# FFN rows of a graph transformer block: stores issued by ScalarE and SyncE instead of by Pool

## What is computed

```python
xn = _layernorm(x)
x = x + gnn(xn, edges) + mix(xn)          # two attentions, 16 heads each
y = _layernorm(x)
q, k, v = (_fff(y, *w[f]) for f in "qkv")  # three routed feed-forward nets
x = x + softmax(q @ k.T / sqrt(1024)) @ v
# _fff: a tree of depth 4 gives each row one of 16 leaves;
# hidden = relu(y @ w1[leaf] + b1[leaf])   (64 wide)
# out    = hidden @ w2[leaf] + b2[leaf]    (1024 wide)
```

## Time and profile before

| | us |
|---|---|
| median of 3 runs | 715.43 (714.16 to 717.3) |
| the profiled execution | 715.37 |
| its span, first to last instruction | 713.6 |
| PE busy | 689.6 |
| DVE busy | 478.7 |
| ACT busy | 404.2 |
| Pool busy | 247.7 |

### The profile page before, as it was taken

How to read it: one execution, slowest core, us unless ns; L and a number is a source line. 1 busy time by engine, 2 the same in 40 slices (tenths; PEclk the granted TensorE clock), 3 DMA queues, 4 the chain that set the end, 5 groups by cost and what they waited for, 6 DMA issues and landing times.

```text
span 713.6 us, 11638 instructions
## 1 busy us (share of the span) xinstructions
PE 689.6 (97%) x4371; PEld 650.6 (91%) x4371; DVE 478.7 (67%) x965; ACT 404.2 (57%) x702; POOL 247.7 (35%) x232
## 2 busy tenths in 40 slices
PE   3999999999999999999999999999999899989998
PEld 3999999998999999999999999998899797879896
DVE  6778756784777477766667565658675667786744
ACT  5655646565565464768686775422432666675541
POOL 5744212122232232127022274564007831252240
PEclk9999999999999999999999999999999999999999
DMA  6822463432333223231313152333168879897342
GB/s 252 314 113 99 198 235 123 175 102 81 121 111 112 99 80 119 96 115 60 118 60 107 72 193 73 130 122 118 60 236 285 303 281 346 325 371 292 117 155 97
DMA packets 25096, 115.38 MB, mean 162 GB/s; under 512 B 7249, under 2 KB 7681, under 8 KB 15969
## 3 DMA queue, kind: packets, MB, share of 16 engines
q1 hardware_dynamic: 14144, 85.05, 32.5%
q0 software_dynamic: 10464, 29.39, 11.7%
q10 hardware_dynamic: 432, 0.20, 0.1%
HBM read 99.35 MB, written 22.49 MB: 171 GB/s over the span
## 4 chain that ended last, share of the span: by engine, by line
PE 85%; DVE 6%; ACT 4%; DMA 3%; issue 1%; ACTq 0%; POOLq 0%; DVEq 0%
PE g_bank L1923 35%; PE g_bank L1948 12%; PE o_bank L2000 5%; PE t_bank L1989 4%; PE s_bank L2280 2%; PE s_bank L1977 2%; PE s_bank L1978 2%; DVE w_lo L1265 2%; PE s_bank L2561 2%; PE s_bank L2508 2%; PE s_bank L2510 2%; PE g_bank L1877 2%; PE s_bank L2509 2%; PE t_bank L2363 2%; PE t_bank L2280 2%; DMA ys<-y_ring 1%
## 5 line engine op out<-in xcount | busy, mean ns | idle before, releaser
L1923 PE MATMUL g_bank<-act_hi,w_hi 128*128 128x384 f32 x488 | 169.3, 347 | 0.2 <-DVE v_st L1292 0.2
L1923 PE MATMUL g_bank<-act_hi,w_lo 128*128 128x384 f32 x488 | 163.6, 335 | 0.0
L1923 PE MATMUL g_bank<-act_lo,w_hi 128*128 128x384 f32 x488 | 163.3, 335 | 0.0
L1265 DVE TENSOR_TENSOR w_lo<-raw,w_hi 128x2048 fp32r<-128x2048 f32 x58 | 135.8, 2342 | 30.2 <-ACT w_hi L777 28.8
L777 ACT ACTIVATE w_hi<-raw 128x2048 fp32r<-128x2048 f32 x67 | 128.2, 1914 | 48.9 <-PE s_bank L2280 12.5
L533 POOL DMA_INDIRECT edge_table<-ew,eidx x51 | 61.0, 1195 | 167.8 <-DMA edge_table<-ew,eidx 163.5
L1923 PEld LDWEIGHTS g_bank<-act_hi,w_hi 128*128 128x128 f32 x488 | 91.8, 188 | 3.1 <-issue 3.0
L1923 PEld LDWEIGHTS g_bank<-act_lo,w_hi 128*128 128x128 f32 x488 | 91.8, 188 | 0.0
L1923 PEld LDWEIGHTS g_bank<-act_hi,w_lo 128*128 128x128 f32 x488 | 91.6, 188 | 0.0
L476 POOL TENSOR_TENSOR w_lo<-raw,w_hi 128x2048 fp32r<-128x2048 f32 x10 | 46.9, 4691 | 99.0 <-ACT w_hi L777 95.0
L1402 DVE TENSOR_TENSOR pT_lo<-t_bank,pT_hi 128x384 fp32r<-128x384 f32 x96 | 50.5, 554 | 33.7 <-ACT pT_hi L870 33.3
(11 more groups left out here) (329 smaller groups left out, 1621.9 us busy)
## 6 DMA issues: line engine op xcount, KB each, us to landing
raw<-wstream_dram SPq DMA_DIRECT2D x68, 1024.0 KB, 4.9
xg<-xs POOLq DMA_DIRECT2D x12, 512.0 KB, 4.6
ys<-y_ring POOLq DMA_DIRECT2D x12, 512.0 KB, 8.0
yv<-y_ring POOLq DMA_DIRECT2D x12, 256.0 KB, 2.3
key_b<-edge_keys SPq DMA_DIRECT2D x1, 1728.0 KB, 10.8
x_sb<-x_dram SPq DMA_DIRECT2D x3, 512.0 KB, 4.9
key_a<-edge_keys SPq DMA_DIRECT2D x1, 1536.0 KB, 6.6
y_acc<-x_dram POOLq DMA_DIRECT2D x3, 512.0 KB, 5.4
```

The source lines that it names most:

```text
L1265: V.tensor_tensor(flat(w_lo[to][:, :, :]), raws[raw_slot(n.base)], flat(w_hi[to][:, :, :]), ALU.subtract) \
L1923: last = mm(out, w2[a], x2[b], start=k == 0 and a + b == 0, stop=not after and k == KT - 1 and a == 1)
```

## The change

Pool no longer issues the stores. The store of a pair of k or q is issued by ACT right behind its own `take_y` of this pair, after a wait for DVE's half. The twelve half stores of v are issued by SP behind its last weight load, each when its half is ready. Pool's program keeps gathers, loads, masks and bias rows in the order before, without the stores between them. Buffers, semaphores and sizes stay.

```diff
@@ sync @@
                 sp.dma_start(raws[raw_slot(n)], wstream[n]).then_inc(raw_in[raw_slot(n)], 16)
+            for i in range(V_PAIRS, V_PAIRS + PAIRS):
+                p = i - V_PAIRS
+                for half in range(2):
+                    sp.wait_ge((y_dve, y_act)[half], i + 1)
+                    sp.dma_start(yv[half][p * P:(p + 1) * P, :], y_at[i][:, half * 512:(half + 1) * 512]) \
+                      .then_inc(v_out[half][p % NT], 16)
@@ gpsimd @@
             load_pair(7)
-            for i in range(PAIRS):
-                store_pair(i)
-            store_pair(PAIRS)
             bias_rows(3)
             stored(0)
             for t in range(NT):
                 bring_k(t)
-            for i in range(PAIRS + 1, 2 * PAIRS):
-                store_pair(i)
-                if i == PAIRS + 1:
-                    load_pair(8)
-                    mask_b1(3)
-                if i == PAIRS + 3:
-                    bias_rows(4)
-                if i > PAIRS + 2:
-                    load_pair(i - PAIRS + 6)
+            load_pair(8)
+            mask_b1(3)
+            bias_rows(4)
+            for i in range(9, 12):
+                load_pair(i)
             bring_back(1)
-            for i in range(V_PAIRS, V_PAIRS + PAIRS):
-                for half in range(2):
-                    store_v(i, half)
             for half in range(2):
                 bring_v(half)
@@ scalar @@
+            def store_y(i):
+
+                f, p = divmod(i, PAIRS)
+                act.wait_ge(y_act, i + 1)
+                act.wait_ge(y_dve, i + 1)
+                act.dma_start(ys[f][p * P:(p + 1) * P, :], y_at[i]).then_inc(y_out[i % NT], 16)
...
                         take_y(PAIRS * b + p)
+                        if b < 2:
+                            store_y(PAIRS * b + p)
```

More of the change, by code:

```diff
@@ L640, in load_sel @@
                 pool.dma_start(sel_g[:, b, :, :], xsel[f].rearrange("(s p) l -> p s l", p=P)).then_inc(sel_in[b], 16)
[L642 to L647, removed]
             def stored(f):
@@ L666, in bring_back @@
                                                  bounds_check=ROWS - 1, oob_is_err=False).then_inc(back_in[t], 16)
[L668 to L673, removed]
             def bring_v(half):
```

## The result

| | before | changed |
|---|---|---|
| median of 20 runs each, us | 714.07 (712.43 to 717.8) | 717.26 (715.07 to 719.09) |
| ratio, 95% interval | | 1.0039 (1.0030 to 1.0049) |
| the profiled execution, us | 715.37 | 716.53 |
| its span, us | 713.6 | 714.6 |
| mean granted clock over the runs (before: four later sets of runs, see below) | 0.997 to 0.998 | 0.996 |

The changed kernel is slower by 0.0039 x 714 = 2.8 us. The forecast was a gain of 2.3 us. A later comparison of the same two kernels gave 1.0053 (1.0036 to 1.0070).

The account below looks back on a forecast made before the run. PE's path was taken as the bound, with only its idle time and slow clock at k's gather winnable. Tile 0.6 us earlier plus 1.7 us of clock made 2.3 us: 715.4 - 2.3 = 713.1 us, range 711.5 to 718.0.

Parts of the forecast that it names:

- Bounds: Whole kernel: PE's path sets the time; only PE's idle time and slow clock around k's gather can be won.
- 2.4 + 1.7 = 4.1 us: At k's first gathered tile: PE's idle time plus the slow clock behind it, all that earlier rows could give.
- early-rows case: Rival at k's gather: store lands in 5 to 6 us, PE waits for nothing; 712.5 to 711.3 us, chance 0.21.
- ACT's stores: k's and q's stores on ACT: 0.6 us each; last k store issued 0.45 us earlier, PE late by 0.9 to 1.4.
- bias wait of the weight load: Sign at 610 us: PE's wait for the bias grows from 0.3 to 0.8 us.
- the idle time ahead of the gather, 2.37 us, hides this whole: Before k's first gathered tile: PE's 0.9 to 1.4 us delay from ACT costs nothing while covered by its idle time.
- Landing of k's last store: k's last store: takes 9.6 - 0.15 us to land; with the earlier issue it lands 0.6 us earlier.
- The gather: Gather of k's rows: still takes 5.2 us, ends 4.5 and 8.0, with more stores beside it.
- the slower rival: At k's gather: stores of pairs 7 and 8 delay it to 629.7; end 718.0, or 719 to 720 us; chance 0.15.
- so there is room: Argument against a slower gather of k's rows: DMA engines moved only 244 GB/s while it ran.
- The clock: Behind k's first gathered tile: about 0.8 us idle keeps PE's clock up, saving 1.7 us; rival that it falls, chance 0.17.
- v's stores, q's gather, copies: Moving v's stores, q's gather and copies waiting for stores: all off PE's path, zero gain.

Follow-up runs that it names:

- e14: Kernel before, Pool's stores kept, with two waits and two tiny activations added on ACT behind each copy of k and q; ratio 1.0024 to before.
- e9: Kernel before, Pool's stores kept, with two waits and a tiny DMA added on ACT behind each copy of k and q; ratio 1.0034 to before.
- e5: Changed kernel with k's and q's stores issued by SP between its weight loads, none by ACT; ratio 1.0021 to the kernel before.
- e12: The changed kernel run once more, unedited; ratio 1.0053 to the kernel before.
- e2: Kernel before with only v's stores moved to SP, k's and q's left on Pool; ratio 1.0006 to before.
- e3: Changed kernel with the stores of pairs 7 and 8 cut to 16 columns; ratio 1.0011 to the kernel before.
- e10: e5 with SP waiting for the first gathered tile ahead of store 7, so later stores come behind the gather; ratio 0.9994 to the kernel before.
- e4: Changed kernel with two weight loads of v's first layer cut to an eighth of their bytes; ratio 0.9990 to the kernel before.
- e13: e5 with two waits and two tiny activations added on ACT behind each copy of k and q; ratio 1.0031 to the kernel before.
- e7: e5 with two weight loads held until the first gathered tile, stores 5 to 8 ahead of the wait; ratio 0.9976 to the kernel before.
- e6: Kernel before with SP holding two weight loads of v's first layer until the first gathered tile has landed; ratio 1.0035 to before.
- e1: Changed kernel with q's stores back on Pool behind the gather, k's on ACT; ratio 1.0051 to the kernel before.

## Why the prediction was wrong

**Bounds.** Right in that the gather's arrival is what ends PE's long wait and that nothing after q's rows moves. Wrong in size: 2.4 + 1.7 = 4.1 us was read from one execution, 1.3 us above the median of 20, in which the clock fell. In other executions it falls less or not at all: a PEclk of 0.58 for 4 us is a stay of (1 - 0.58) x 4 / 0.5 = 3.4 us at 1.2 instead of 2.4 GHz, which lowers the mean by 0.5 x 3.4 / 714 = 0.0024, and of 115 runs of the kernel before in the four sets of experiments 28 had a mean of 0.999 or 1.000. So part of the 1.7 us was not there to win. Nor was this the only place where the clock fell: the profiled execution of before lost as much at 568 to 576 us (0.74 and 0.83), ahead of all that the change touches, the changed kernel's nothing there. A small slip without effect: the range is said to begin at the middle of the early-rows case, which is 711.9, and begins at 711.5.

**ACT's stores.** Right for a single one: 0.33 us of issue and 0.46 us between the copy and ACT's next instruction (0.45 forecast for the issue, 0.6 for what a store takes of ACT in all; no run shows the 0.15 us added for the copy to drain). k's last store is issued 0.47 us earlier from the start of the layer, 0.45 forecast. PE arrives 1.64 us later, 0.9 to 1.4 forecast. The bias wait of the weight load grew from 0.29 to 0.82, as forecast (0.3 to 0.8); half of the delay, 0.77 us, is a wait for ACT's selections at 614.00 that no step named. Wrong was "the idle time ahead of the gather, 2.37 us, hides this whole". e14 and e9 cost 1.7 and 2.4 us with every store where it was. The cover was no independent one: k's last store hangs on a copy that ACT makes behind the same work, so what delays PE delays the idle time's end too.

**Landing of k's last store.** Forecast 0.15 us shorter, measured 2.4 shorter, and 0.4 to 3.0 shorter in four other kernels whichever engine issued it (Pool 6.62 in e14, 8.11 in e9; SP 9.22 in e5; ACT 8.37 in e12). So the issuing queue does not set it. It agrees with the Trainium skill ("DMA: Bandwidth & Descriptors", section "Issuing engines are not separate DMA queues") that issuing from another engine saves only the issue time, as do the medians of 8.1 and 8.0 us.

**The gather: the step that failed.** "I take 5.2, the ends being 4.5 and 8.0" measured 10.18 and 10.54. The argument against the slower rival was that the DMA engines moved only 244 GB/s in 624 to 628, "so there is room". The same row gives their busy share as 0.92: few bytes, but hardly any free time. That stretch carried few bytes because the weight loads of 620 had ended by then and because Pool's blocked queue held stores 7 and 8 back; the change moved the gather 2.9 us forward and the stores beside it, into 620 to 628 at 420 and 409 GB/s. e2 (8.25 us in the old order, issued early) shows that a gather issued early takes longer, e3, e10 and e4 that the company makes it longer still. The sum had store and gather as two terms that do not touch, 9.46 and 5.2; together they are one, and it measured 18.4 us instead of 15.8. With the store issued 0.5 us earlier that is the 2.1 us by which the tile was later. The rival, one megabyte ahead of the gather at 325 GB/s, priced this at a landing of 629.7 instead of 627.04, 2.7 us later, and at 718.0 in all; the tile was 2.1 us later from the start of the layer and the median is 717.26. This rival was the right account in its main part, it had 0.15, and the range reached to it. The rule named beside it, that the DMA engines take the queues in turn ("DMA: Bandwidth & Descriptors", section "Queues, rings and completion order", of the Trainium skill), would lengthen a gather with each busy queue beside it. The gather took 10.18 and 10.54 us with the stores in ACT's queue and 8.53 and 8.97 (e5, e13) with the same stores in SP's, one busy queue fewer, which agrees; the time of store and gather together (18.4 and 19.9 against 18.7 and 18.3) does not tell them apart, and no run here shows the turns themselves.

**The clock.** "I take it that the clock then stays up" had no chance to be seen, as the idle time did not shrink (2.83 us). In the changed kernel's 20 runs and the 6 of e12 none had a mean clock of 0.998 or more; of the 115 of before 66 had. The means, 0.9956 against some 0.997, differ by 0.0015: about 1.1 of the 2.8 us. How much of this lies at the gather and how much at 568 to 576, where 14 of the 16 profiled executions lost the clock too, a mean cannot say: a profiled execution with one short loss had 0.997 or 0.998, one with both losses 0.995, but e12 with one long loss at the gather (0.51 and 0.64 over 8 us) had 0.995 too.

**v's stores, q's gather, copies.** All right: zero (e2), zero, and waits for landed stores off PE's path.

**Where the 2.8 us are.** e5, all of the change but ACT, costs 1.5 us, and with stores 7 to 11 behind the gather again (e10) nothing; ACT's work costs 0.7 us on top (e13) or 1.7 alone (e14). 1.5 + 0.7 to 1.7 makes 2.2 to 3.2. The clock's 1.1 us is within these, not beside them. With ends that wide the split is a rough one.

## What to carry to other kernels

A queue that stands blocked behind a gather also works as a priority: it keeps later transfers out of the way of the one that is due first. Where DMA engines are full, look up what each transfer to be moved would run beside before giving it a free queue, and take a transfer's length from the stretch in which it will run. Of two transfers in a row on full DMA engines, price the pair, not each. Idle time covers an added delay only if its end does not hang on the same engine; and of transfers with slack, hold back the loads (e7), but only if what they then collide with has slack too (e6).

## What was not expected of the hardware

The clock did not follow the length of the idle time alone. e2's PE stood still for 2.47 us and e1's for 2.63 us, and neither lost the clock. The busy time by stretch of e2 behind its idle time:

```profile
628.00:632.00 4.00, 4.00 (x24) 3.36 (x22) 2.16 (x3) 3.05 (x4) 2.85 (x4) 1.00 1.03 408
```

The kernel before lost it after 2.37 us (0.58 in the same stretch), the changed kernel after 2.83, e14 after 2.21 (0.61). But for e1, whose PE had the first gathered tile behind it, PE did the same work in the same order before it stood still. And at 568.6 to 569.0 us, in a part that the change does not touch, PE had stood still for 2.56 us in the kernel before, which lost the clock (0.74, then 0.83), and for 2.57 us in the changed kernel, which kept it at 1.00. Why some executions keep the clock stays open.

The same gather of 384 rows took 5.2 us in the profiled execution of before and 10.5 us in e12. Stores of 512 KB took 6.6 to 9.6 us for k's last pair in kernels in which little else differs around it. The sum of the two was steadier than either: 15.3 to 16.6 us in ten kernels.
